# A two-layer graph kernel: the first layer's weights applied to x before the neighbour sum, instead of to the sum afterwards

## The reference

```python
# layer 0
deg = clip(sum(adj, axis=1) + 1, 1, None)
h_neigh = (adj @ X + X) / deg
z = concatenate([X, h_neigh], axis=1) @ W + b        # W is 128 x 64
out = relu(z)
out = out / maximum(norm(out, axis=1), 1e-12)
x = layernorm(x + out)
# layer 1
neigh = adj @ x / (sum(adj, axis=1) + 1)
x = layernorm(x + concatenate([x, neigh], axis=-1) @ W1.T)
```

## Time and profile before

| | |
|---|---|
| median of 3 runs | 790.53 us (790.47 to 792.68) |
| profiled execution | 794.09 us, span of its instructions 792.3 us |
| PE busy | 697.7 us, 88% of the span |
| DVE busy | 709.1 us, 90% |
| ACT busy | 621.0 us, 78% |
| POOL busy | 201.7 us, 25% |
| adj, x and weights read | 270.6 MB, 344 GB/s over the span |
| mean granted TensorE clock | 0.946 |

### The profile page before, as it was taken

The page is one execution under the profiler, slowest core; times in us unless marked ns, Lnnn a source line. Parts: engine busy times, 40 slices in busy tenths (PEclk is TensorE's granted clock), DMA queues, the critical chain, the costliest instruction groups (busy, mean ns, idle before and its releaser), DMA issues.

```text
span 792.3 us, 28217 instructions
## 1 busy us (share of the span) xinstructions
PE 697.7 (88%) x11285; PEld 638.3 (81%) x11285; DVE 709.1 (90%) x2687; ACT 621.0 (78%) x848; POOL 201.7 (25%) x302
## 2 busy tenths in 40 slices
PE   1477868888898889999999999999999999999992
PEld 0467757777787778888889989899999989889992
DVE  4699977989999999999999999989999989878894
ACT  4798887989898989898988889787878889740037
POOL 2262513535413133334222030201102020201024
PEclk9988896989999999999999999999999999999997
DMA  9999999999999999999999999999999999800004
GB/s 304 388 419 419 419 419 401 408 420 410 421 417 416 415 416 395 421 393 421 390 417 385 404 381 393 372 344 384 345 411 361 404 350 368 314 2 2 2 15 96
DMA packets 46121, 274.56 MB, mean 347 GB/s; under 512 B 12642, under 2 KB 12706, under 8 KB 13218
## 3 DMA queue, kind: packets, MB, share of 16 engines
q1 hardware_dynamic: 45184, 270.55, 86.3%
q0 software_dynamic: 576, 2.10, 0.7%
q10 hardware_dynamic: 226, 0.07, 0.0%
HBM read 270.60 MB, written 2.10 MB: 344 GB/s over the span
## 4 chain that ended last, share of the span: by engine, by line
PE 48%; DVE 29%; issue 8%; DMA 6%; POOL 5%; ACT 3%; ACTq 0%; DVEq 0%; POOLq 0%; SPq 0%
PE s_ps L360 22%; DVE e L737 10%; PE u_ps L378 7%; DVE t_sb L744 6%; PE p_ps L346 6%; DMA a_in<-in_adj 3%; POOL small L1088 3%; PE z_ps L396 3%; DMA xl<-in_x 3%; PE z_ps L393 3%; PE z_ps L417 2%; DVE u_sb L744 2%; PE u_ps L428 1%; PE p_ps L428 1%; DVE a_in L744 1%
## 5 line engine op out<-in xcount | busy, mean ns | idle before, releaser
L542 ACT ACTIVATE junk<-a_in 128x2048 uint8<-128x2048 uint16 x256 | 489.2, 1918 | 4.0 <-DMA a_in<-in_adj 4.0
L360 PE MATMUL s_ps<-xh,t_sb 128*128 128x129 f16 x4096 | 386.7, 250 | 18.6 <-DVE t_sb L744 15.5
L360 PEld LDWEIGHTS s_ps<-xh,t_sb 128*128 128x128 fp8e4 x4096 | 311.3, 102 | 48.4 <-DVE t_sb L744 19.4
L737 DVE TENSOR_SCALAR e<-a_in 128x2048 fp8e4<-128x2048 f32 x256 | 310.2, 1222 | 8.2 <-DMA a_in<-in_adj 7.7
L1096 POOL COPY store<-pk 128x32 uint32<-128x32 uint32 (+1 forms) x250 | 119.8, 521 | 313.2 <-ACT pk L551 313.2
L346 PE MATMUL p_ps<-pow_bf,e 128*128 128x16 bf16 x4096 | 142.5, 170 | 51.7 <-DVE e L737 48.8
L346 PEld LDWEIGHTS p_ps<-pow_bf,e 128*128 128x128 fp8e4 x4096 | 128.6, 97 | 68.8 <-DVE e L737 62.7
L744 DVE TENSOR_SCALAR t_sb<-pk 128x128 uint32<-128x128 uint32 x1024 | 150.8, 219 | 6.5 <-ACT pk L551 6.0
L1088 POOL TENSOR_TENSOR small<-small,minus_half 128x4 f32<-128x4 f32 x32 | 65.3, 2040 | 228.0 <-DVE small L798 176.4
L378 PE MATMUL u_ps<-xh,u_sb 128*128 128x128 f16 x1488 | 99.1, 218 | 0.0
L378 PEld LDWEIGHTS u_ps<-xh,u_sb 128*128 128x128 fp8e4 x1488 | 88.9, 97 | 1.2
(11 more groups left out here) (102 smaller groups left out, 512.6 us busy)
## 6 DMA issues: line engine op xcount, KB each, us to landing
a_in<-in_adj SPq DMA_DIRECT2D x256, 1024.0 KB, 8.9
xl<-in_x POOLq DMA_DIRECT2D x4, 512.0 KB, 15.8
out_h<-e SPq DMA_DIRECT2D x8, 256.0 KB, 2.6
w_sb<-in_L_gnn_W ACTq DMA_DIRECT2D x1, 32.0 KB
w_raw<-in_L_gnn_W ACTq DMA_DIRECT2D x1, 32.0 KB
b_sb<-in_L_gnn_b ACTq DMA_DIRECT2D x1, 0.2 KB
```

Source lines behind the costliest of these rows:

```text
L360: last = nc.tensor.matmul(s_ps[:, n % 2, at:GW], t_sb[:, b, :], xh[:, b, at:GW], start=(b == 0), stop=False)
L542: nc.scalar.activation(junk[:, t % 2, :], halves[t % R], ACT.Copy, scale=1.0 / 128, accum_out=half_sum[:, n, c:c + 1]).then_inc(s_half, 1)
L737: nc.vector.tensor_scalar(e8[:, c, :], a_in[:, t % R, :], 1.0, None, ALU.is_equal, saturate=False).then_inc(s_e, 1)
```

## The change

The neighbour sum and the weights of layer 0 are both linear, so (adj @ x + x) @ W_low is (adj + I) @ (x @ W_low). The kernel after computes, once for each of the 64 row blocks of x, a product with a 65 x 128 matrix `wy_sb`: its left half holds the upper half of W with the bias in the 65th row, its right half the lower half of W times 2048. The left result goes to `acc`, the right one is split into `y_hi` and `y_lo`, which take the place of `x_hi` and `x_lo` in the neighbour sum. This is done in block 1, in 16 groups of four blocks: PE transposes (`transpose_x`) and multiplies (`dense_x`), ACT copies the transposed blocks and `y_hi` (`take_xs`), DVE copies `acc` and subtracts for `y_lo` (`split_y`).

The batch epilogue loses `transpose_cat`, `take_cat`, `dense` and `take_z`. `layer1` on DVE now does what `mean` and `norm` did, and the relu: sum times 1/deg plus `acc`, then a max with zero. The steps behind it are moved forward: `residual` and `normalise` into k = 2, `transpose_h` into (2, 3), `dense_h` to the start of k = 3, with POOL's roots and ACT's copies moved with them. ACT issues three more small transfers at the start (weights and bias once more), all engines' start waits for them, `weights()` moves from block 1 to block 2, the guards from blocks 2 to 5 to blocks 3 to 6. The wait for the first layer-1 features of a new segment stands at the quarter that needs it.

```diff
@@ tensor
+            def transpose_x(g):
+                pe.wait_ge(s_x[g * NC // NE], 16)
+                if g >= 2:
+                    pe.wait_ge(s_xt, g - 1)
                 for k in range(BR):
-                    last = nc.tensor.transpose(c_ps[:, k, :], xl[:, e * BR + k, :], ident[:, :])
-                last.then_inc(s_catps, 1)
+                    last = nc.tensor.transpose(xt_ps[g % 2][0:F, k, :], x_sb[:, g * BR + k, :], ident[:, :])
+                last.then_inc(s_xtps, 1)
+
+            def dense_x(g):
+                pe.wait_ge(s_xt, g + 1)
+                if g >= 2:
+                    pe.wait_ge(s_ylo, g - 1)
+                for k in range(BR):
+                    last = nc.tensor.matmul(y_ps[g % 2][:, k, :], x_t[:, g % 2, k, :], wy_sb[:, :],
+                                            start=True, stop=True)
+                last.then_inc(s_yps, 1)
...
-                if e >= 0 and k == 2:
-                    dense(e)
+                if e >= 0 and k == 3:
+                    dense_h(e)
                 for c in range(NC):
                     pack_chunk(n, c)
-                    if e >= 0 and (k, c) == (1, 3):
-                        transpose_cat(e)
+                    if n == 1:
+                        for g in range(c * NE // NC, (c + 1) * NE // NC):
+                            if g == 0:
+                                transpose_x(0)
+                            if g + 1 < NE:
+                                transpose_x(g + 1)
+                            dense_x(g)
+                    if e >= 0 and (k, c) == (2, 3):
+                        transpose_h(e)
...
             tail_sums(0)
-            transpose_cat(e)
             tail_sums(1)
-            dense(e)
             tail_sums(2)
+            transpose_h(e)
             tail_sums(3)
-            transpose_h(e)
+            dense_h(e)
             tail_sums(4)
-            dense_h(e)
@@ scalar
+            def take_xs(c):
+                for g in range(c * NE // NC, (c + 1) * NE // NC):
+                    if g == 0:
+                        take_xt(0)
+                    if g + 1 < NE:
+                        take_xt(g + 1)
+                    take_y(g)
@@ vector
+            dve.wait_ge(s_w, 96)
+            nc.vector.tensor_scalar(wy_sb[0:F, F:2 * F], wy_sb[0:F, F:2 * F], YS, None, ALU.mult).then_inc(s_wy, 1)
+            def split_y(c):
+                for g in range(c * NE // NC, (c + 1) * NE // NC):
+                    rows = slice(g * BR, (g + 1) * BR)
+                    dve.wait_ge(s_yhi, g + 1)
+                    nc.vector.tensor_copy(acc[:, rows, :], y_ps[g % 2][:, :, 0:F])
+                    nc.vector.tensor_tensor(y_lo[:, rows, :], y_ps[g % 2][:, :, F:2 * F], y_hi[:, rows, :],
+                                            ALU.subtract).then_inc(s_ylo, 1)
...
-                nc.vector.tensor_tensor(acc[:, rows, :], s_sb[:, :, :], bc(small[:, 0, :], BR),
-                                        ALU.mult).then_inc(s_mean, 1)
-            def norm(e):
-                dve.wait_ge(s_r, e + 1)
+                for k in range(BR):
+                    ins = nc.vector.scalar_tensor_tensor(out=z_sb[:, k, :], in0=s_sb[:, k, :],
+                                                         scalar=small[:, 0, k:k + 1], in1=acc[:, e * BR + k, :],
+                                                         op0=ALU.mult, op1=ALU.add)
+                link(ins)
+                link(nc.vector.tensor_scalar(r_sb[:, :, :], z_sb[:, :, :], 0.0, None, ALU.max))
...
             for n in range(NB):
                 e, k = n // BR - 1, n % BR
                 compare(n, 0)
+                if n == 1:
+                    split_y(0)
                 if n:
                     unpack(n - 1, 0)
-                if e >= 0 and k == 3:
-                    normalise(e)
                 if n > START[1]:
                     add_piece(n - 1)
+                if e >= 0 and k == 2:
+                    residual(e)
                 compare(n, 1)
-                if n == 0:
-                    split_x(0)
+                if n == 1:
+                    split_y(1)
                 if n >= START[1]:
                     unpack_piece(n)
-                if e >= 0 and k == 2:
-                    norm(e)
+                if e >= 0 and k == 3:
+                    low_part(e)
+                    begin_acc(e)
                 compare(n, 2)
-                if n == 0:
-                    split_x(1)
-                    split_x(2)
+                if n == 1:
+                    split_y(2)
                 if n:
                     unpack(n - 1, 1)
                 if e >= 0 and k == 1:
-                    mean(e)
+                    layer1(e)
+                if e >= 0 and k == 2:
+                    normalise(e)
                 compare(n, 3)
+                if n == 1:
+                    split_y(3)
@@ gpsimd
                 if e >= 0 and k == 2:
-                    root(0, e)
+                    root(1, e)
                 if n:
                     keep(n - 1)
-                if e >= 0 and k == 2:
-                    root(1, e)
+                if e >= 0 and k == 1:
+                    root(0, e)
```

## The result

The change takes 816.05 us (median of four executions, 812.80 to 821.96). Of the kernel before, four executions ran beside it: three took 790.47 to 792.68 us, median 790.53, and one took 1243.40, which no comparison here uses. Against the three the change takes 1.032 times as long, interval 1.024 to 1.040. The forecast was 797.5 us, the range 786 to 811; the time lies outside it. The profiled execution took 812.80 us with a span of 811.0 and is the fastest of the four. Against the profiled execution before (span 792.3) it is 18.7 us longer, where the sum had +7.0.

A forecast was written before the change was run, and what follows sets the result against it. It took DMA to pace blocks 2 to 11, DVE blocks 12 to 35, and PE, with DVE close behind, the late blocks. +30.7 - 5.0 - 15.4 - 3.3 = +7.0 us on the 790.5 median gave 797.5, range 786 to 811.

The forecast's parts named there:

- Block 2's start: Products on x in block 1, begun at 24 us, move block 2's start from 40.0 to 70.7 us: +30.7.
- the gaps: Between block 1's quarters engines wait for each other, 11.4 us in all; PE idles 1.5 to 2.5 us in each.
- The clock term: Block 1: PE's 29.6 us of work at a mean granted clock of 0.82 adds 6.5 us.
- A group at full clock: Block 1: PE sets the pace inside a quarter, 1.57 us per group (transposes 0.48, product 1.09).
- The weights' small transfers: At the start, they hold PE and DVE back until about 11 us, hidden by the fifth chunk; uncovered, 2 us.
- Blocks 2 to 11: With six chunks already loaded, engines run at their own pace, 97.7 us instead of 102.7: -5.0.
- Blocks 12 to 63: DVE's 25.8 us of waits go and 13 x 0.8 us of work comes, leaving 547.9 us: -15.4.
- Tail: PE paces until about 750 us and loses the concatenation's transposes (0.48) and dense product (2.90): -3.3.
- (a): Rival: half clock through all of block 1, block 2 at 84.3 us, +20.6, 811 us; chance 0.16.
- (b): Rival: full clock in block 1 with the gaps, block 2 at 64.2 us, +0.5, 791 us; chance 0.16.
- the forecast's gains of 23.7 us: After block 2's start: -5.0 in blocks 2 to 11, -15.4 in blocks 12 to 63, -3.3 in the tail.
- (c): Rival: block 1's quarters run into each other, block 2 at 56.7 us, -7.0, 783.5 us; chance 0.18.

The follow-up runs named there:

- e4: The change itself, unaltered, timed once more beside the other runs: 818.1 us.
- e3: The change, with the epilogue's residual, normalise, transposes, dense product and ACT copies back in their old places: blocks 36 to 63 take 314.4 us against 319.1.
- e8: The change without the products on x and with the epilogue's steps in their old places; output not the reference's: 778.8 us.
- e5: The change plus unread 8-bit products on PE ahead of block 1's codes, at quarter ends and in each group: 808.6 us.
- e2: The change, with DVE comparing the next chunk ahead of the quarter's split: profiled execution 822.8 us, fastest 804.5.
- e9: The change with old epilogue places, x's first quarter behind block 0's last codes, and quarters running into each other: 800.7 us.
- e11: Quarters running on and old places, plus unread fill products and the first two groups' transposes ahead of block 0's last codes: 793.9 us.
- e12: e11 with only the 64 neighbour columns multiplied ahead of the sums, the own half in the batch epilogue: 813.7 us.
- e7: The change with x's products in block 0, old epilogue places and unread fill products before and in the groups: block 2 starts at 76.4 us.
- e1: The change without the products on x, new epilogue and its order kept; output not the reference's: 782.6 us.

## Why the prediction was wrong, by its own steps

The sum was +7.0 us; the profiled execution shows +18.7 and the medians +25.5.

**Block 2's start, +30.7 forecast.** It was +31.1. The start at 24 us (24.6), and the gaps (2.34, 1.25, 2.33 us of idle PE, where 1.5 to 2.5 were forecast) came near enough. The rest fits by luck, through two errors that cancel. The clock term of 6.5 us was a mean over a thing with two levels: half clock until 42 us, full until 60, half again. Eight of the sixteen groups went at 2.56 us instead of 1.34, which is 9.8 us (an estimate, 8 x 1.22), 3.3 more than forecast. A group at full clock takes 1.34 us and not 1.57, since records overlap, which is 3.7 less over sixteen. Another execution of the same kernel (e4) had block 2 at 74.3. The weights' small transfers landed later than worked out, at 15.8 us instead of 11, and were hidden as the forecast said, by the wait for the fifth chunk:

```profile
...
15.83 0.19 DVE L715 TENSOR_SCALAR wy_sb<-wy_sb 64x64 f32<-64x64 f32 x1 [9.91 <-DMA wy_sb<-in_L_gnn_b]
...
24.60 1.23 DVE L758 TENSOR_SCALAR e<-a_in 128x2048 fp8e4<-128x2048 f32 x1 [3.67 <-DMA a_in<-in_adj]
...
```

**Blocks 2 to 11, -5.0 forecast.** -3.7.

**Blocks 12 to 63, -15.4 forecast. This is the step that failed.** It read: "I therefore take the waits on r_sb, g_hi and the late pk as gone", with DVE's pace as its busy time and nothing else. The stage took 566.4 us instead of 570.0: -3.6, and 11.8 us of the forecast are missing, as much as the sum is off the profiled execution. The old waits did go (25.8 to 2.3), and PE's work in blocks 36 to 63 did shrink (321.0 to 298.4 us, 22.6 where 23.7 was forecast). What failed is that this time would come out of the stage.

In blocks 12 to 35 the old waits had been 7.3 us only. DVE's busy time grew by 3.1 there (236.58 to 239.69), new waits for chunks of 2.7 came, and the stage did not get shorter by more than 0.6 us in any run (246.2 us at the least, 246.8 before). The transfers leave little room there, which the earlier trace rows had shown: their share is 1.01 in blocks 12 to 35 as in blocks 2 to 11, and a block takes 10.28 us (246.8 / 24) where it took 10.27 (102.7 / 10). The forecast read only the step from 416 to 412 GB/s and had DVE alone pace. In e3's blocks 12 to 35 ACT, too, waits for chunks, which it didn't before:

```profile
...
ACT junk L562 <- DMA a_in<-in_adj: 10.6, 20, 1.2
...
```

No run changes the transfers, so this bound is read from the rows and not tested.

In blocks 36 to 63 DVE's busy time grew by 4.5 and the waits moved: residual now stood ahead of compare 1, PE idled for it (18.3 us), and DVE in turn waited for PE's catch-up at add_piece (8.4 us). e3 and e8 show the place as the cause of these two waits: with the old places the stage is 314.4 and 313.8 us. The prediction had named this bound ("If DVE's waits did not go but moved, the 15.4 would shrink towards zero") and gave it no chance. The place is only a part of what is missing: with the old places blocks 12 to 63 take 561.2 to 562.9 us in seven kernels, 7 to 9 less than before where 15.4 was forecast. In e8's row DVE is busy for 302.7 of 313.8 us, and from 323.2 before that is 9.4 us in all. What the other 11.1 us of DVE's idle time wait for was followed only for g_hi (4.6 us).

```profile
...
388.50:702.30 313.80, 295.95 (x4831) 269.02 (x4828) 302.68 (x1190) 256.63 (x327) 44.48 (x67) 1.00 0.91 362
...
```

**Tail, -3.3 forecast.** -5.1; PE is busy for 59.3 us there instead of 64.3.

**Beyond the profile, +6.8.** The other executions of the change are slower than the profiled one, and those of the kernel before are not. The forecast added its sum to a median as if both had the same spread. e5 points at the clock: with the clock held in block 1 the executions lie within 1.5 us. What the clock did in the longer executions of the change is not shown, since only the shortest has a profile.

**Rivals.** (a), half clock through all of block 1, is nearly what e2's profiled execution shows (822.8 us, fourteen groups of sixteen), and (a) may be what the longer executions of the change, at 818 to 824 us, are; it had been given 0.16. The waits in the section of the Trainium skill that the prediction cites for it ("TensorE: Matmul & The Clock Gate", section "HAM oscillation — how this bites in real kernels") are for transfers and longer than any gap in block 1. Those are 2.34 us at most, so by that section (a) did not follow. (b), full clock with the gaps, had the forecast's gains of 23.7 us behind it. e5, at full clock in all of block 1, is 17 us slower than before, and some 10 without its groups' fill (16 x 0.45, an estimate), so with the gains as they are (b) does not reach no change. (c), quarters that run into each other, needed a rewritten order: e9 and e11.

## What to carry to other kernels

A wait that is removed by moving a step is worth its length only if the engine behind the new place isn't made to wait: before counting it, name what the moved step now stands ahead of on its engine, and who reads that. Work added ahead of a pipeline cost its length here in both blocks where it was tried; what helped was an early start and letting its parts run into each other. Where the transfers are busy for a whole stage, as in blocks 12 to 35 here, expect little of an engine's shorter waits, and read their share next to the engines'. Where a stage of float32 matmuls can run at two levels of the clock, forecast two times with chances, not a mean, and look at more than one execution.

## What the runs showed of the hardware that I had not expected

A float32 product of 64 columns costs as much as one of 128 (1.06 us for eight records either way). From the start of the eight records to what follows them it is 0.90 us in both (35.71 to 36.61 in e11, 36.53 to 37.43 in e12). The loads of the stationary operand, which has 128 columns in both kernels, are as long too, 0.97 us for eight, first e11, then e12:

```profile
...
35.61 0.97 PEld L401 LDWEIGHTS z_ps<-wy_sb,agg 65*128 65x128 f32 x8
...
```

```profile
...
36.48 0.97 PEld L402 LDWEIGHTS z_ps<-wy_sb,agg 65*128 65x128 f32 x8
...
```

The Trainium skill ("TensorE: Matmul & The Clock Gate", section "LDWEIGHTS (loading the stationary operand)") has a load's time set by the columns of the stationary operand alone. By its figure eight loads are an estimated 0.85 us, near the 0.90 of these rows. The estimate doesn't fit at half the clock, where the same eight products are 1.71 us from start to what follows (33.33 to 35.04 in the change). That the load is the bound here was not tested by itself.

PE kept at half the clock for 48 us of nearly unbroken float32 work in e2, and at full clock in e5 with 8-bit products between the same float32 ones; in e7 the same fill in each group, without that at the quarters' ends, did not hold it behind 54 us. What decides is left open.

POOL's operations got slower in the new order (in e1 too, which has no products on x: 692 and 2764 ns), by the groups of lines (busy us, mean ns of one, idle before), first of the change, then of e3 with the old places:

```profile
...
L1115 POOL COPY store<-pk 128x32 uint32<-128x32 uint32 (+1 forms) x250 | 171.6, 729 | 371.2 <-ACT pk L571 371.2
L1107 POOL TENSOR_TENSOR small<-small,minus_half 128x4 f32<-128x4 f32 x32 | 88.5, 2765 | 131.3 <-DVE small L819 66.7 <-DVE small L836 64.6
...
```

```profile
...
L1115 POOL COPY store<-pk 128x32 uint32<-128x32 uint32 (+1 forms) x250 | 110.3, 484 | 377.2 <-ACT pk L571 377.0
L1107 POOL TENSOR_TENSOR small<-small,minus_half 128x4 f32<-128x4 f32 x32 | 66.4, 2075 | 181.9 <-DVE small L836 110.5 <-DVE small L819 71.4
...
```

The root takes 2765 ns instead of 2075, and the copy 729 instead of 484, for the same shapes and counts. No engine waited for POOL, so it cost nothing; what slowed it was not tried.
